# The tail of a mixture-of-experts and Mamba kernel: five blocks over all tokens against one block over two halves of them

## The reference

```
h   = acc                                   # gelu(x_n @ w_in + b_in) + forward Mamba + backward Mamba
n   = (h - mean(h)) * rsqrt(var(h) + eps) * ln_g + ln_b
x   = x + n @ w_out.T + b_out
y   = layernorm(x)
out = x + (silu(y @ gate.T) * (y @ up.T)) @ down.T      # 688 hidden units
```

## Time and profile before

| | |
|---|---|
| median of 3 runs | 1210.09 us (1208.47 to 1212.72) |
| the profiled execution, its own time | 1213.12 us |
| its span in the profile | 1211.4 us |
| mean granted TensorE clock in it | 0.936 of full speed |
| busy share | PE 85%, DVE 72%, ACT 47%, POOL 60% |
| scans and their set-up (block at L1283) | 548.2 to 1112.2 us |
| tail, from there to the end | 99.2 us |

### The profile page before, as it was taken

One profiled execution on the slowest core, in us unless ns is written; L12 is line 12 of the kernel. 1 busy time (PEld: TensorE's weight loads), 2 busy tenths in 40 slices (PEclk: granted clock), 3 DMA queues, 4 the chain that ended last, 5 costly groups with the idle time before them and its releaser, 6 DMA issues. The chain is left out here.

```text
span 1211.4 us, 13540 instructions
## 1 busy us (share of the span) xinstructions
PE 1023.8 (85%) x4008; PEld 638.8 (53%) x4008; DVE 874.1 (72%) x1082; ACT 563.7 (47%) x1164; POOL 721.8 (60%) x510
## 2 busy tenths in 40 slices
PE   6889866999999999967869876988898886865598
PEld 2566655888888888854324332433353232312376
DVE  4577746777777777772079789878987899895732
ACT  1666632334434443423555775556555664542230
POOL 1255531566556656635079787978897889892100
PEclk9899976999999999987979888998899999999799
DMA  3000023342443234220235555554554455560001
GB/s 104 1 1 0 1 86 111 121 126 86 121 121 121 91 113 130 78 72 20 55 94 154 148 148 135 147 125 134 142 141 132 139 137 152 147 161 0 1 1 35
DMA packets 60591, 116.04 MB, mean 96 GB/s; under 512 B 10832, under 2 KB 15952, under 8 KB 60416
## 3 DMA queue, kind: packets, MB, share of 16 engines
q1 hardware_dynamic: 59408, 113.61, 33.5%
q10 hardware_dynamic: 1136, 1.90, 0.5%
HBM read 113.98 MB, written 1.51 MB: 95 GB/s over the span
## 5 line engine op out<-in xcount | busy, mean ns | idle before, releaser
L1331 POOL TENSOR_TENSOR uB<-u,rows_B 128x512 f32<-128x512 f32 x256 | 319.4, 1274 | 26.9 <-DVE da L1445 26.9
L768 POOL TENSOR_TENSOR lutw<-lutw,lt 128x860 f32<-128x860 f32 x80 | 200.0, 2500 | 149.6 <-DVE lt L745 143.9
L1459 PE MATMUL ya<-hV,ident 128*128 128x512 f32 x336 | 194.5, 665 | 78.4 <-DVE hV L1406 78.0
L1445 DVE TENSOR_TENSOR_SCAN da<-da,uB 128x512 f32<-128x512 f32 x168 | 201.1, 1220 | 28.8 <-ACT da L1387 21.2
L1459 PEld LDWEIGHTS ya<-hV,ident 128*128 128x128 f32 x336 | 61.9, 203 | 179.0 <-DVE hV L1406 140.6
L1340 POOL TENSOR_TENSOR hP<-hS,rows_C 128x512 f32<-128x512 f32 x88 | 111.9, 1271 | 31.4 <-DVE hS L1442 14.4
L1442 DVE TENSOR_TENSOR_SCAN hS<-da,uB 128x512 f32<-128x512 f32 x88 | 106.8, 1214 | 21.7 <-ACT da L1386 9.4
L1386 ACT ACTIVATE da<-zero 128x2 f32<-128x2 f32 x256 | 43.2, 169 | 157.7 <-DVE hV L1406 155.4
L1406 DVE TENSOR_TENSOR hV<-da,rows_C 128x512 f32<-128x512 f32 x168 | 112.4, 670 | 0.0
L723 ACT ACTIVATE ah<-ups 128x1024 fp32r<-128x1024 f32 x40 | 41.2, 1030 | 121.7 <-DVE ups L741 121.7
L1459 PE MATMUL ya<-hP,ident 128*128 128x512 f32 x176 | 92.6, 608 | 0.0
(11 more groups left out here) (251 smaller groups left out, 2140.1 us busy)
## 6 DMA issues: line engine op xcount, KB each, us to landing
rows_B<-bc_rows SPq DMA_DIRECT2D x128, 256.0 KB, 3.6
rows_C<-bc_rows SPq DMA_DIRECT2D x128, 256.0 KB, 4.3
wr<-in_moe_w SPq DMA_DIRECT2D x41, 384.0 KB, 4.1
cwb<-cw_rows SPq DMA_DIRECT2D x16, 512.0 KB, 4.1
cwb<-cw_rows SPq DMA_DIRECT2D x16, 384.0 KB, 5.0
cwb<-cw_rows SPq DMA_DIRECT2D x16, 256.0 KB, 3.8
lut_f<-in_lut_idx SPq DMA_DIRECT2D x1, 2144.0 KB, 8.5
cwb<-cw_rows SPq DMA_DIRECT2D x16, 128.0 KB, 3.7
```

The source lines that it names most:

```text
L768: e.tensor_tensor(part, part, lt[:, q, :], ALU.add).then_inc(s_la, 1)
L1331: e.tensor_tensor(uB[:, n % UBUF, :], u[:, seg % 2, d, :], RB[:, q, :], ALU.mult).then_inc(s_ub, 1)
L1445: e.tensor_tensor_scan(a[:, way], a[:, way], uB[:, n % UBUF, way], 0.0, ALU.mult, ALU.add).then_inc(s_sc, 1)
L1459: return e.matmul(ya[n % 2][:, :], g.ident[:, :], at, start=False, stop=False, skip_group_check=True).then_inc(done, 1)
```

## The change

Four edits. (1) `routing` also folds the layernorm into the weights: `gw` is `w_out` scaled by `ln_g` (ScalarE, two activations of 256 columns), the mean of its columns comes from two fp32 matmuls, and `w_out` becomes `gw` minus that mean, so that a product with raw sums comes out free of the mean; two more activations and two more matmuls add `ln_b`'s part to `b_out`. (2) At the head of GpSimd's program in `mamba`, `b_out` is added to `x`. (3) Half of the last segment's projection is made between scan steps (`last_out_tensor`), the two feature chunks in two banks `LB` = S2 and S0, so only four matmuls are left behind the last gates. (4) The five blocks are replaced by one, `finish`: for each half of the tokens PE transposes `acc` and multiplies it by the new `w_out`; the transposes serve only for the statistics. The inverse root comes from ScalarE's Ln and Exp and a Newton step. The table's low parts are made on GpSimd. The feed-forward runs over 12 steps of 512 tokens (six row blocks of the first half, six of the second), and the second half's sums, layernorm and transposes stand between the first half's steps.

```
@@ -563,6 +565,14 @@
                         mm = e.matmul(lps[:, n, :], g.feat[:, k, n * P:(n + 1) * P], wt.gate[:, k, :],
                                       start=k == 0, stop=k == KC - 1)
                 mm.then_inc(s_lg, 1)
+                e.wait_ge(s_gw, KC)
+                e.wait_ge(s_1d, 1)
+                for k in range(KC):
+                    e.matmul(wps[:, 0, :], mean[:, :], gw[:, k, :], start=k == 0, stop=k == KC - 1)
+                e.wait_ge(s_of, KC)
+                for k in range(KC):
+                    mm = e.matmul(wps[:, 1, :], off[:, k, :], wt.w_out[:, k, :], start=k == 0, stop=k == KC - 1)
+                mm.then_inc(s_wp, 1)
                 e.wait_ge(s_cw, 1)
                 e.wait_ge(s_pr, 2)
                 for n in range(NB):
@@ -606,12 +616,18 @@
+                e.wait_ge(s_wp, 1)
+                e.tensor_tensor(wt.w_out[:, :, :], gw[:, :, :], wps[:, 0:1, :].broadcast_to([P, KC, D]),
+                                ALU.subtract).then_inc(s_wo, 1)
+                e.scalar_tensor_tensor(wt.b_out[:, :], wps[:, 1, :], float(D), wt.b_out[:, :], ALU.mult,
+                                       ALU.add).then_inc(s_wo, 1)
                 e.wait_ge(s_tp, 1)
                 e.tensor_copy(ex.cwT[:, :], tps[:, :]).then_inc(s_te, 1)
                 ex.split_low(e, 0, 1)
 
             @block.gpsimd
...
@@ -619,6 +635,12 @@
             def _(e):
+                e.wait_ge(wt.late_in, wt.late_n)
+                for k in range(KC):
+                    e.activation(gw[:, k, :], wt.w_out[:, k, :], ACT.Identity, scale=wt.ln[:, 0, k:k + 1]).then_inc(s_gw, 1)
+                e.wait_ge(s_1d, 1)
+                for k in range(KC):
+                    e.activation(off[:, k, :], mean[:, :], ACT.Identity, scale=wt.ln[:, 1, k:k + 1]).then_inc(s_of, 1)
                 ex.split_high(e, 0, 16)
                 e.wait_ge(s_sh, 1)
@@ -1044,10 +1067,33 @@
+        def last_out_tensor(e):
+            k = NSEG - 1
+            w = ws[k // 2]
+            yield 46
+            e.wait_ge(s_g, DB * k + 2)
+            e.wait_ge(s_oa, KC * k)
+            for m in range(KC):
+                for q in range(2):
+                    e.matmul(LB[m][:, :], w.out[:, q, m * P:(m + 1) * P], sz[:, k % 2, q, :], start=q == 0, stop=False,
+                             skip_group_check=True)
+                    yield 47 + 2 * m + q
+            yield NEVER - 1
+            for q in range(2, DB):
+                e.wait_ge(s_g, DB * k + q + 1)
+                for m in range(KC):
+                    mm = e.matmul(LB[m][:, :], w.out[:, q, m * P:(m + 1) * P], sz[:, k % 2, q, :], start=False,
+                                  stop=q == DB - 1, skip_group_check=True)
+                    if q == DB - 1:
+                        mm.then_inc(s_om, 1)
+
         def side_tensor(e, seg):
...
@@ -1251,7 +1297,8 @@
-                e.tensor_tensor(acc[:, m, half_of(k)], S2[:, :], acc[:, m, half_of(k)], ALU.add).then_inc(s_oa, 1)
+                from_bank = LB[m] if k == NSEG - 1 else S2
+                e.tensor_tensor(acc[:, m, half_of(k)], from_bank[:, :], acc[:, m, half_of(k)], ALU.add).then_inc(s_oa, 1)
 
         def softplus(e, k, d):
@@ -1303,6 +1350,8 @@
 
             @block.gpsimd
             def _(e):
+                e.tensor_tensor(g.x[:, :, :], g.x[:, :, :], wt.b_out[:, :].unsqueeze(1).broadcast_to([P, NB, D]),
+                                ALU.add).then_inc(s_res, 1)
                 e.memset(raw[:, :, :, 0:PADC], 0.0).then_inc(s_pad, 1)
                 e.memset(raw[:, :, :, PADC + SEQ:], 0.0).then_inc(s_pad, 1)
@@ -1498,163 +1547,268 @@
+def finish(c, g, out, wt, acc):
...
+        xn = c.sb(ctx, "ff_xn", [P, NB, D])
+        pt = [c.ps(ctx, f"fo_t{h}", [P, HB, D]) for h in range(NH)]
+        pz = [c.ps(ctx, f"fo_z{h}", [P, HB, D]) for h in range(NH)]
+        flat = lambda ap: ap[:, :, :].rearrange("p n d -> p (n d)")
+        turned = [flat(p).rearrange("p (k t) -> p k t", k=KC) for p in pt]
+        gate_up = [[flat(p)[:, i * HALF:(i + 1) * HALF] for i in range(2)] for p in (pz[0], pt[0])]
+        down = [pz[1], pt[1]]
+        blocks = lambda h: slice(h * HB, (h + 1) * HB)
+        half_of = lambda h: slice(h * HALF, (h + 1) * HALF)
         with nc.Block() as block:
             @block.tensor
+                def turn(h):
                     for k in range(KC):
+                        for n in range(HB):
+                            e.wait_ge(s_xn, h * HB + n + 1)
+                            mm = e.transpose(turned[h][:, k, n * P:(n + 1) * P], xn[:, h * HB + n, k * P:(k + 1) * P],
+                                             g.ident[:, :])
+                        mm.then_inc(s_tp, 1)
...
+                def gates(i):
+                    h, m = tables[i]
+                    o, r = FB[m]
+                    if m == 0:
+                        e.wait_ge(s_lo, KC * (h + 1))
+                    if i >= 2:
+                        e.wait_ge(s_a, i - 1)
+                    for j, (wh, wl, sem) in enumerate(((gh, gl, s_g), (uh, ul, s_u))):
+                        terms = [(w, x, k) for w, x in ((wh, xh), (wh, xl), (wl, xh)) for k in range(KC)]
+                        for t, (w, x, k) in enumerate(terms):
+                            if i == 0 and t == 2 * KC:
+                                e.wait_ge(s_ll, j + 1)
+                            mm = e.matmul(gate_up[i % 2][j][0:r, :], w[:, k, o:o + r], x[:, k, half_of(h)],
+                                          start=t == 0, stop=t == len(terms) - 1)
+                        mm.then_inc(sem, 1)
...
+                for h in range(NH):
+                    for n in range(HB):
+                        at = slice((h * HB + n) * P, (h * HB + n + 1) * P)
+                        for k in range(KC):
+                            mm = e.transpose(pt[h][:, n, k * P:(k + 1) * P], acc[:, k, at], g.ident[:, :])
                     mm.then_inc(s_t, 1)
+                    for n in range(HB):
+                        at = slice((h * HB + n) * P, (h * HB + n + 1) * P)
+                        for k in range(KC):
+                            mm = e.matmul(pz[h][:, n, :], acc[:, k, at], wt.w_out[:, k, :], start=k == 0, stop=k == KC - 1)
+                    mm.then_inc(s_z, 1)
+                turn(0)
+                for i in range(len(tables)):
+                    gates(i)
+                    if i == 3:
+                        turn(1)
+                    if i == M + 1:
+                        down_half(0)
+                down_half(1)
+            @block.vector
+            def _(e):
+                def variance(l, h, count, done):
+                    e.wait_ge(s_bs, count)
+                    for n in range(h * HB, (h + 1) * HB):
+                        e.bn_aggr(mv[:, l, n, :], st[:, l, n, :]).then_inc(s_ag, 1)
+                    e.wait_ge(s_ag, done * HB)
+                    e.tensor_scalar(va[:, l, blocks(h)], mv[:, l, blocks(h), 1], EPS, None, ALU.add).then_inc(s_va, 1)
+                def inverse(l, h, count):
...
+                def sums_stats(h):
+                    e.wait_ge(s_t, h + 1)
+                    for n in range(HB):
+                        e.bn_stats(st[:, 0, h * HB + n, :], pt[h][:, n, :]).then_inc(s_bs, 1)
+                def output(h):
+                    e.wait_ge(s_z, h + 1)
+                    for n in range(HB):
+                        b = h * HB + n
+                        e.scalar_tensor_tensor(g.x[:, b, :], pz[h][:, n, :], ri[:, 0, b:b + 1], g.x[:, b, :],
+                                               ALU.mult, ALU.add).then_inc(s_x, 1)
+                        e.wait_ge(s_x, b + 1)
+                        e.bn_stats(st[:, 1, b, :], g.x[:, b, :]).then_inc(s_bs, 1)
...
+                def normal(h):
+                    for b in range(h * HB, (h + 1) * HB):
+                        e.tensor_scalar(xn[:, b, :], g.x[:, b, :], mv[:, 1, b, 0:1], ri[:, 1, b:b + 1],
+                                        ALU.subtract, ALU.mult).then_inc(s_xn, 1)
...
+                sums_stats(0)
+                variance(0, 0, HB, 1)
+                sums_stats(1)
+                inverse(0, 0, 1)
+                output(0)
+                variance(1, 0, 3 * HB, 2)
+                variance(0, 1, 3 * HB, 3)
+                inverse(1, 0, 2)
+                normal(0)
+                inverse(0, 1, 3)
+                low_x(0)
+                output(1)
+                variance(1, 1, 4 * HB, 4)
+                act(0)
+                act(1)
+                low(0)
+                inverse(1, 1, 4)
+                normal(1)
+                for i in range(2, len(tables)):
+                    act(i)
+                    low(i - 1)
+                    if i == 3:
+                        low_x(1)
+                    if i == M + 3:
+                        result(0)
+                low(len(tables) - 1)
+                result(1)
             @block.scalar
...
```

(19 more changed lines are left out.)

237 lines of the change are left out of this document (104 added, 133 removed).

## The result

The changed kernel took 1191.61 us (median of 4 runs, 1190.21 to 1192.22) beside 1210.05 us for the kernel before, a ratio of 0.9844 with a 95% interval of 0.9824 to 0.9864. Run again later beside the kernel before, the same kernel gave 1190.99 against 1211.23 us, 0.9828 (0.9815 to 0.9841). It is faster by 18 to 20 us; forecast were 26, and the time lies 1.6 us above the range.

The account below looks back on a forecast made before the run. PE was taken to bound the FFN, with 40.0 us before it in which engines work one after the other. Terms 0 + 3.5 - 5.3 - 22.4 - 0.7 - 1.3 = -26.2 took 1210.09 to 1183.9 us, range 1179.5 to 1190.

Parts of the forecast that it names:

- Routing, 0: In routing, the added matmuls, VectorE operations and ScalarE activations fit into idle time and cost 0.
- The addition at the head of the Mamba block, +3.5: GpSimd's 4.56 us addition delays the diagonals and PE's first projection; with the clock's effect, +3.5 us.
- Rival A: At the Mamba block's start the addition is hidden, PE's start hanging on something else: 1180.4 us, chance 5%.
- the 1.1 us that the forecast had the clock give back: At PE's first Mamba projection, a low-clock loss of 2.9 us becomes 1.8, so the 4.56 us delay costs 3.5.
- End of the scans, -5.3: After the last gates only four projection matmuls remain, the others moving into PE's waits between scan steps: -5.3 us.
- Complete sums to the first FFN matmul, -22.4: Between complete sums and the first FFN matmul, 17.6 us for 40.0, GpSimd slowing VectorE by nothing: -22.4 us.
- FFN, -0.7: In the FFN, same matmuls, 1.0 us of transposes added, a PE wait of about 1.8 nearly gone: -0.7 us.
- Rival C: Through the FFN's 12 steps the clock stays low, slower than before: 1232 us, chance 2%.
- Output, -1.3: After the last matmul, four additions and four stores instead of eight, 3.7 for 4.9 us: -1.3 us.
- From the span to the time: Whole kernel: the sum is made on the span (1185.2 us) and its difference taken off the median, giving 1183.9 us.
- B: In the early FFN steps VectorE's second-half work starves PE at steps 3 to 5: 1187 to 1190 us, chance 20%.
- D: From sums to normalised tokens VectorE's chain is longer, 0.2 us more per some 25 small operations: 1189 us, chance 8%.

Follow-up runs that it names:

- the last one: Reordered kernel (GpSimd's addition moved, low parts waiting, VectorE taking first half's outputs earlier) plus 20 and 12 unread transposes in TensorE's waits: 1178.64 us, ratio 0.9728.
- the kernel with both repairs: Changed kernel with GpSimd's b_out addition behind its Mamba matrices and its table low parts waiting for VectorE's small operations: 1180.31 us, ratio 0.9758.

## Why the prediction was wrong

**Routing, 0.** Right. The two new VectorE operations took 0.68 and 0.42 us, and VectorE's copy of `cw`, at 191.89 us in the earlier trace rows, starts at 191.80.

**The addition at the head of the Mamba block, +3.5.** The size came out (+3.4) and the path is right: PE's first projection starts at 564.99 us for 560.83, released by the diagonals as foretold. Rival A falls. The kernel with the addition behind the matrices took it back. But the 1.1 us that the forecast had the clock give back did not come from there, so that part is luck. From the first projection to VectorE's first operation of the scans are 43.2 us for 43.1; what came back lies in the scans (496.9 us for 497.8). In the seven profiled executions with the addition at the head, the last segment's first gate comes 556.7 to 556.9 us after the start of the block five times and 559.2 us twice, for 553.2 to 553.5 us in three executions of kernels without it: +3.3 to +6.0.

**End of the scans, -5.3.** Right: 5.17 us for 10.46, and 5.18 in the kernel where this is the only edit.

**Complete sums to the first FFN matmul, -22.4.** This step failed: -19.4. In its words, "I price no slowing", since the operations beside GpSimd "read PSUM or one tile of SBUF". That held for the large ones and was wrong for the Newton step's and the variance's: `fo_ri<-fo_ri,fo_qq` reads two inputs in SBUF, and `fo_va<-fo_mv`, with one input, has input and output in SBUF, so "one tile of SBUF" was no safe sign either. Two faults lie in it. The list of what runs beside GpSimd left out the operations that are cheap by themselves; but what is paid here is the remaining length of the other engine's operation, whatever the size of one's own. And the alternative was priced as a slowing ("1.6 times"), from an average over four operations of which one had stood for 3.3 us and three had not. Held back, GpSimd costs this stretch nothing and it is 17.45 us: the rest of the working, some thirty operations, was right to 0.2 us, and so it was on the way (the second transposes end 5.72 us after the last addition for 5.85, the normalised half is there 14.65 us after it for 14.75).

The Trainium skill has the rule, on a page other than the one the forecast cited: "SBUF — State Buffer", section "SBUF: two separate sides", says that VectorE and GpSimd share a pair of ports as an exclusive lock, held for a whole instruction by whichever starts first, against VectorE operations of two SBUF inputs or in a two-port mode, while the other "fully blocks". The traces of this stretch agree: 2.84 and 3.08 us with whole subtractions, 0.82 to 0.84 us with pieces of 0.88, 0.17 us with none, and 0.47 us either way for the operation that reads PSUM. In the Mamba block they agree in part only (last section). The row of the Trainium skill that the forecast cited ("GPSIMD Engine Reference", Specifications) calls the same thing contention, and "by it the sum stays" was a wrong reading even so: it names two SBUF inputs, which `fo_ri` has.

**FFN, -0.7.** Measured +0.25. The steps are as foretold (2.78 us each, 0.87 for the second half's transposes, no wait of PE). Two parts were mis-sized. PE's wait between the up and the down products, now gone, was priced at 1.8 us; it was 1.2 (in the kernel before PE's matmuls start every 0.12 us there, and the gap is 1188.49 to 1189.83 us). And the low clock at the start was taken to cost 1.8 us on both sides: the thirteenth matmul starts 4.89 us after the first, for 2.89 at the full clock, a loss of 2.0 us, where the kernel before lost 1.5. (The 5.06 us in the chain run to the end of the twelfth.) The table loads cost PE nothing; the one at 1138.50 us took 1.28 us, the next activation starting 1.30 after it. The Trainium skill's 2.66 us for a switch ("ScalarE: Activation LUTs", What ACT_TABLE_LOAD costs) is not what this trace shows. Rival C, the clock low throughout, falls.

**Output, -1.3.** Measured -0.9, from 4.94 to 4.06 us.

**From the span to the time.** The five terms missed by 4.3 us in sum; the other 3.4 us are the last step. It took the profiled execution for 3.0 us above the median (1213.12 against 1210.09) and gave the changed kernel the same excess. But the changed kernel's profiled execution was at its median (1191.23 and 1191.61), and the kernel before came out at 1211.1 to 1211.5 in three later batches. Executions of one kernel differ by some 5 us, and three runs place a median no better than to 1 or 2. An error of this size belonged into the range: 1180 to 1188 took the terms' bounds and nothing for this step.

**Rivals B and D.** B did not come in the changed kernel, only in the last one. D gave nearly the right time (1189) for a wrong reason: it spread 5 us over 25 small operations, and the trace has two operations that are 5.6 us too long and cost the stretch 3.2.

## What to carry to other kernels

Before work goes to GpSimd beside a chain of VectorE, list every VectorE operation in that window, the 0.2 us ones first, and see which have their operands in SBUF alone; each may cost what is left of GpSimd's operation. (May: the statistics operation has them there and did not stand.) Place GpSimd's operations beside VectorE's work on PSUM, with a wait if need be, and put none at the head of a block where something waits behind it. And where a group's total looks like sharing, read its shortest and longest member before dividing by the count.

## What the runs showed of the hardware

A VectorE operation of 0.16 us of work can stand for the whole rest of a GpSimd operation (it took 3.08 us), and cutting GpSimd's work into pieces makes the next small operations stand in turn, 0.83 us each.

It can be GpSimd that stands. At the head of the Mamba block GpSimd's matrices take 0.60 us each when VectorE is idle. Where VectorE subtracts two tiles in SBUF, VectorE keeps its 0.69 us and a matrix takes up to 1.32. From the kernel before, two pairs of matrices (0.60 and 0.60, then 0.60 and 1.16 us) and the subtraction beside the second pair:

```profile
551.86 1.18 POOL L1312 TENSOR_SCALAR conv_diag<-ident,fm_cvw 128x128 f32<-128x128 f32 x2
554.48 1.74 POOL L1312 TENSOR_SCALAR conv_diag<-ident,fm_cvw 128x128 f32<-128x128 f32 x2
```

```profile
555.05 0.69 DVE L1420 TENSOR_TENSOR hl<-acc,hh 128x512 fp32r<-128x512 f32 x1 [1.02 <-ACT hh L1352]
```

Another subtraction began at 553.34 us, inside a matrix that ended at 553.62, and neither was longer than usual. So short operations need not exclude each other for their whole length. Which engine stands, and for how long, is better read from a trace than assumed.

The granted clock fell to 0.50 (1.2 GHz) around idle times of TensorE as short as 1.7 and 1.4 us with 2.1 us of transposes between them, and stayed at 1.00 when waits of 0.42 and 0.34 us were left there. But the length of one idle time does not settle it: in the kernel with both repairs PE was idle for 3.21 us ahead of its first projection, and the clock stayed at 1.00.

```profile
559.34:566.00 6.66, 5.88 (x19) 3.56 (x20) 0.16 (x1) 1.20 (x2) 6.66 (x9) 1.00 0.00 0
```

The same clock explains a part of the spread between executions. The changed kernel, and the same kernel run again, over the first 6.4 us from PE's first projection on:

```profile
564.99:568.60 3.61, 2.90 (x6) 1.79 (x6) 0.00 (x0) 0.58 (x1) 3.61 (x7) 0.50 0.00 0
568.60:571.40 2.80, 2.73 (x7) 2.15 (x8) 0.00 (x0) 0.01 (x1) 0.88 (x2) 0.50 0.00 0
```

```profile
565.94:569.55 3.61, 2.90 (x6) 1.79 (x6) 0.00 (x0) 0.58 (x1) 3.61 (x7) 0.55 0.00 0
569.55:572.35 2.80, 2.73 (x9) 1.81 (x10) 0.00 (x0) 0.61 (x2) 0.89 (x2) 1.00 0.00 0
```

In the first the clock stays at half for the second stretch too, and VectorE's first operation of the scans comes 43.2 us after the first projection; in the second it comes after 41.6. Over all profiled executions this takes 40.3, 41.6, 43.1 or 44.1 us, with PE's work the same. The Mamba block itself starts between 546.2 and 548.7 us. Neither is set by the edits alone: kernels with the same program there have different values. What decides which value an execution gets wasn't tried. A change of under 3 us in this kernel is better read from its own stage than from the time.
